# A macaron transformer block on one core: FFN pieces dealt out over the attention rounds by two tables, and the output projection in other PSUM banks

## The reference

```
x = x + 0.5 * ffn(layernorm(x))
x = x + attn(layernorm(x))
x = x + 0.5 * ffn(layernorm(x))

ffn(x)  = (silu(x @ w_gate.T) * (x @ w_up.T)) @ w_down.T          # hidden 2048
attn(x): q, k, v = x @ w_qkv                                      # 16 heads of 32
         q, k = unit norm per head, rope on every other head
         logits = q @ k.T * q_gain, causal mask
         y = softmax(logits) @ v;  return y @ w_out
```

## Time and profile before

| | |
|---|---|
| median of 3 runs | 2855.55 us (2854.16 to 2855.95) |
| the profiled execution | 2854.06 us, of it 2852.1 us from the first to the last instruction |
| PE busy | 2760.0 us, 97% of the span |
| DVE, ACT, POOL busy | 1755.9, 1206.4, 527.0 us |
| granted TensorE clock, mean | 0.995 |
| start of the first `qkv` of rounds 0 to 7 | 189.7, 479.2, 796.2, 1110.0, 1451.9, 1793.8, 2135.7, 2422.0 us |
| start of their second halves | 359.8, 646.1, 947.8, 1286.7, 1628.6, 1970.5, 2302.6, 2593.0 us |

### The profile page before, as it was taken

The page is one execution under the profiler, slowest core; times in us unless marked ns, Lnnn a source line. Parts: engine busy times, 40 slices in busy tenths (PEclk is TensorE's granted clock), DMA queues, the critical chain, the costliest instruction groups (busy, mean ns, idle before and its releaser), DMA issues.

```text
span 2852.1 us, 56217 instructions
## 1 busy us (share of the span) xinstructions
PE 2760.0 (97%) x23232; PEld 2025.0 (71%) x23232; DVE 1755.9 (62%) x4158; ACT 1206.4 (42%) x2250; POOL 527.0 (18%) x820
## 2 busy tenths in 40 slices
PE   5999999999999999999999999999999999999999
PEld 4677766776677776777767777677767766777676
DVE  7765666666656565566656566565656666665643
ACT  5443444354434443444434444344443444344422
POOL 0012132213130301213021120302103031303100
PEclk8999999999999999999999999999999999999999
DMA  6000000000000000000000000000000000000000
GB/s 253 1 16 1 16 1 1 1 16 16 1 1 16 16 1 1 1 16 16 1 1 16 1 16 1 1 16 16 1 16 1 16 1 1 1 16 9 1 9 15
DMA packets 16574, 39.37 MB, mean 14 GB/s; under 512 B 1472, under 2 KB 1472, under 8 KB 15808
## 3 DMA queue, kind: packets, MB, share of 16 engines
q1 hardware_dynamic: 16320, 35.79, 3.5%
HBM read 26.35 MB, written 9.44 MB: 13 GB/s over the span
## 4 chain that ended last, share of the span: by engine, by line
PE 84%; DVE 10%; ACT 3%; issue 2%; POOL 1%; DMA 0%; SPq 0%; ACTq 0%; DVEq 0%
PE psum L1034 24%; PE psum L1036 24%; PE psum L1035 24%; PE psum L1186 2%; PE psum L1163 2%; DVE mneg L928 2%; PE psum L1198 1%; PE psum L1145 1%; DVE arena L876 1%; PE psum L1141 1%; DVE arena L878 1%; PE psum L1057 1%; DVE arena L949 1%; DVE arena L871 1%; PE psum L1164 1%
## 5 line engine op out<-in xcount | busy, mean ns | idle before, releaser
L1034 PE MATMUL psum<-arena,WG 128*128 128x256 f16 x2048 | 559.1, 273 | 4.9 <-DVE arena L878 3.4
L1036 PE MATMUL psum<-arena,WG 128*128 128x256 f16 x2048 | 559.3, 273 | 0.0
L1035 PE MATMUL psum<-arena,WG 128*128 128x256 f16 x2048 | 559.1, 273 | 0.0
L1034 PE MATMUL psum<-arena,WU 128*128 128x256 f16 x2048 | 558.4, 273 | 0.0
L1036 PE MATMUL psum<-arena,WU 128*128 128x256 f16 x2048 | 558.3, 273 | 0.0
L1035 PE MATMUL psum<-arena,WU 128*128 128x256 f16 x2048 | 558.3, 273 | 0.0
L876 DVE SCALAR_TENSOR_TENSOR arena<-arena,psum 128x256 f32<-128x256 f32 x512 | 215.1, 420 | 492.2 <-ACT arena L768 491.2
L768 ACT ACTIVATE arena<-psum,tscale 128x256 f32<-128x256 f32 x512 | 241.9, 472 | 633.1 <-PE psum L1036 632.8
L1034 PE MATMUL psum<-WD,arena 128*128 128x512 f16 x1024 | 388.1, 379 | 3.9 <-DVE arena L882 3.8
L1036 PE MATMUL psum<-WD,arena 128*128 128x512 f16 x1024 | 388.0, 379 | 0.0
L1035 PE MATMUL psum<-WD,arena 128*128 128x512 f16 x1024 | 387.9, 379 | 0.0
(11 more groups left out here) (147 smaller groups left out, 4534.6 us busy)
## 6 DMA issues: line engine op xcount, KB each, us to landing
arena<-in_L_attn_x SPq DMA_DIRECT2D x16, 512.0 KB, 3.8
out<-arena SPq DMA_DIRECT2D x16, 512.0 KB, 2.8
arena<-in_L_ffn_w_gate SPq DMA_DIRECT2D x4, 1024.0 KB, 9.3
arena<-in_L_ffn_w_up SPq DMA_DIRECT2D x4, 1024.0 KB, 7.3
WD<-in_L_ffn_w_down SPq DMA_DIRECT2D x4, 1024.0 KB, 12.3
arena<-in_L_attn_w_qkv SPq DMA_DIRECT2D x1, 3072.0 KB, 22.1
...
```

The costliest lines, as they stand in the source:

```text
L1034: T_.matmul(o, lhs(0), rhs(0), start=first, stop=False)
L1035: T_.matmul(o, lhs(0), rhs(1), start=False, stop=False)
L1036: return T_.matmul(o, lhs(1), rhs(0), start=False, stop=last)
```

## The change

Two things are changed.

1. `projections`, `heads` and `out` take a table w with a number of beats for each of their places, instead of constants. Rounds 0, 1, 6 and 7 (`SHORT`) use `FEW`, the others `MANY`. Before, the heads' places had 1 beat (0.8 in rounds 0 and 7), the prelude's 0.4 of that, the places of the projections 1, 3 (after the last tile) and 2. The stages themselves, their number and their sequence inside the attention are the same; `max_group` only gathers three lines that stood twice.
2. The output projection writes tiles 0 to 3 into banks 2, 0, 1, 2 (`OUT_BANK`) and not 0, 1, 2, 0. The first `qkv` of a round waits for two out residuals before its first matmul and for the third before its 13th (the v part, in bank 1). The `stack turn` that next uses bank 2 now waits for the fourth.

```
-    LOAD, LEFT, PACE, PRELUDE, SCARCE, ENDS = 9, 3, (0, 2, 3, 4), 0.4, 0.8, 3
+    LOAD, LEFT, PACE = 9, 3, (0, 2, 3, 4)
+    SHORT = (0, 1, 6, 7)
+    MANY = {"qk": 1.88, "qk first": 1, "ends": 3, "stack": 2, "v first": 1.25, "turned": 1, "max first": 0.4,
...
+    FEW = {"qk": 1, "qk first": 2, "ends": 2.4, "stack": 2, "v first": 1, "turned": 1, "max first": 0.32,
...
-                fill(1)
+                fill(w["qk"] if t else w["qk first"])
...
-                    fill(ENDS)
+                    fill(w["ends"])
...
         def attention(b):
+            w = FEW if b in SHORT else MANY
             for hf in range(2):
-                projections(b, hf)
-                heads(b, hf, SCARCE if b in (0, B - 1) else 1)
-            out(b)
+                projections(b, hf, w)
+                heads(b, hf, w)
+            out(b, w)
...
+    OUT_BANK = (2, 0, 1, 2)
...
-                V_.scalar_tensor_tensor(out=x_t, in0=ps(t % 3), scalar=unscale[:, 2:3], in1=x_t, op0=ALU.mult, op1=ALU.add).then_inc(s["x2_done"], 1)
+                V_.scalar_tensor_tensor(out=x_t, in0=ps(OUT_BANK[t]), scalar=unscale[:, 2:3], in1=x_t, op0=ALU.mult, op1=ALU.add).then_inc(s["x2_done"], 1)
...
                 elif b:
-                    pe.wait_ge(s["x2_done"], TT * b)
+                    pe.wait_ge(s["x2_done"], TT * (b - 1) + 2)
...
+                if b and hf == 0 and t == 0:
+                    pe.wait_ge(s["x2_done"], TT * (b - 1) + 3)
...
-                if t == 2:
-                    reader[2] = "x2_done", TT * b + 3
+                if t == 3:
+                    reader[2] = "x2_done", TT * b + 4
```

60 lines of the change are left out of this document (31 added, 29 removed).

## The result

| | before | after |
|---|---|---|
| median | 2855.19 us (2854.16 to 2855.95, 4 runs) | 2815.77 us (2814.85 to 2817.38, 4 runs) |
| profiled execution | 2854.06 us, span 2852.1 | 2815.85 us, span 2814.0 |
| PE busy | 2760.0 us, 97% | 2749.1 us, 98% |

The changed kernel takes 0.9862 of the time of the kernel before (95% interval 0.9849 to 0.9876). Of all executions in this document one, of e13, ran at a mean clock of 0.944 and took 2911 us; it is left out.

A forecast was written before the change was run, and what follows sets the result against it. PE, busy 97% of the span, was taken as the bound, leaving its 92 us of idle time and low-clock time to win; terms 6.6 + 4.4 + 8.0 + 2.5 + 0 + 1.4 - 1.9 + 1.7 = 22.7 us gave 2833 us, range 2825 to 2848.

The forecast's parts named there:

- Term 1: Turns of the rounds: six waits of the first qkv for the fourth out residual go, gain 6.6 us.
- Rival B: First qkv at the turns: another late release takes the out residual's place, term 1 lost, 2839.5 us; chance 0.05.
- Term 2: Stack turns in short rounds' second halves: two pieces instead of one remove four waits, gain 4.4 us.
- Term 3: Preludes of short rounds' second halves: residual and norm leave DVE's queue there, PE's waits shrink, gain 8.0 us.
- Terms 4 and 5: Single waits behind layer norms, 2.5 us; heads: 0 to 3 gain 0 on a straight line, 4 to 7 gain 1.4.
- the lower bound: Heads 0 to 3 of the four short rounds: all 2.8 us of idle time gone in each, -11 us.
- term 6: Long rounds: two places in the first half's prelude lose their only piece, costing 1.9 us.
- Term 4's last sentence: Waits of values for a turn's split: four before, four after at other heads, so nothing gained.
- Term 7: Round 1's second half: the one clock fall goes as two waits that meet are moved apart, gain 1.7 us.
- Rival C: Short rounds' first halves: short waits gather and bring more stretches at 1.2 GHz, 2841.5 us; chance 0.06.
- A: Heads 0 to 3, short rounds' first halves: 25 pieces too few to cover DVE, +11 us, 2844 us; chance 0.15.
- D: Heads 0 to 3, four first halves: DVE becomes the bound, 41 us lost, slower kernel at 2874 us; chance 0.05.

The follow-up runs named there:

- e13: Changed kernel with the short rounds' weight for values and values' turns at 0.769 instead of 0.56, exponentials kept at 1.2; 2836.64 us, 0.9939 of the kernel before.
- e1: Kernel before with only the output projection's new banks and the two changed waits, pieces placed as before; 2845.52 us, 0.9968 of the kernel before.
- e5: Changed kernel with other short-round head weights: similar piece counts per group of heads, placed elsewhere inside each head; 2831.1 us, 0.9918 of the kernel before.
- e7: Changed kernel with the short rounds' head weights all 0.3 (18 pieces in heads 0 to 3) and projections at old values; 2866.3 us, 1.0042 of before.
- e4: Changed kernel with the short rounds' six head weights all set to their mean, 0.769; 2837.85 us, 0.994 of the kernel before.
- e10: Changed kernel with more beats for the v part in all rounds (FEW 2, MANY 1.9); 2818.06 us, 0.9873 of the kernel before.

## Why the forecast was right in sign and short in size

**Term 1, the banks: right.** 6 x 1.10 us was the price, 6.6 us the gain, in the changed kernel and in e1. Rival B is out.

**Term 2, the stack turns: right, for half a reason.** The four waits went, 4.4 us; small ones beside them bring it to 5.9. I had reasoned with one piece of 1.23 us against a wait of 1.0 at the last place. Three halves of e13 have that piece and wait all the same: the wait is for the whole way from the last `qkv` over `stack` to `stack turn`, and the pieces on that way count, six before and in e13, eight after. They are there because the first halves took fewer, not because the table says 2.

**Term 3, the preludes: the mechanism right, 1.2 us too much.** DVE's load went where the order said. What is left is 2.0 us in the four (1.2 by the second count), where I had left one wait of 0.31 in three of them. By the second count 8.1 us were there to win and not 8.9: the eight waits were priced too high.

**Terms 4 and 5, the heads: here the forecast failed.** Forecast 3.9 us, measured 14.7, and with that 2815.8 us and not 2833. The step is "on a straight line between the two rows the halves would share the 2.8 us". Two rows, 33 pieces with 0 us idle and 16 with 2.8, do not give a line. What PE loses there is a number of single waits, and each ends when the place ahead of it has enough pieces; 2 pieces were nearly enough ahead of the scores and 1 too few ahead of the next `scores max`, as the table of pieces and e5 show. Both halves therefore end near zero (0.35 and 0.09 us idle in round 6; over the four short rounds 13.2 us lost became 6.2): I had that case as the lower bound, -11 us, and took the middle for no better reason than that it was the middle. The range cut part of that bound off. In heads 4 to 7 I had priced the pieces of round 7 and four single waits, some 3 us, and added nothing for the small waits of the other halves; 7.6 us were won there. Of PE's waits before, those of `y turn` (2.2 us in six) and of `values` for the low halves (1.8 us in four) are not in its list after; what each place of heads 4 to 7 gained was not tried by itself. The two terms make 10.8 of the 16 us by which the gain was forecast too small, term 6 makes 4.2.

**Term 4's last sentence, "four before, four after: nothing", was wrong too.** The four waits of `values` for a split are four, but take 2.6 us and not 4.8. A count of places is not a sum of waits: what stands on DVE ahead of the split sets the length.

**Term 6, the long rounds: wrong sign, a misread order.** I wrote that two places of the first half's prelude lose their only piece. They do not: ahead of the second, third and fourth `scores max` stood 2, 1, 2 pieces, and now 1, 2, 1. The window of round 4's first prelude after shows no idle time.

```profile
1504.30:1518.30 14.00, 14.00 (x116) 10.12 (x115) 9.58 (x26) 2.86 (x6) 0.00 (x0) 1.00 0.00 1
```

What I did not look for is in the heads: the wait of `max rows` for a split, 0.70 us in the second half of each of the four rounds, went, and heads 0 to 3 of both halves won 3.6 us; 1.8 were lost in the second halves' projections, to norm turns. Term 6 should have been +2.3.

**Term 7, the clock: the right sum, by luck.** The 1.7 us came, but e1 gets them with the two waits still together. What decides on a fall stays open. The Trainium skill (TensorE: Matmul & The Clock Gate, section "A second HAM failure mode: psum-queue depth-cycling") says that a PE which idles briefly again and again can swing between the clocks. The traces agree as far as they go: e7, with 81.6 us lost, has five falls of 3.41 us each between 600 and 2700 us, the kernel before with 70.3 has one, the changed kernel none. But the number of falls does not follow the loss alone: e4 and e13, with over 50 us lost, have none, e10 with some 34 has two. Rival C did not come: the changed kernel has no fall between 65 us and its end.

**Rivals A and D** stood on DVE's mean share. A asked for 11 us in the four first halves, which lost 1.8 us more in heads 0 to 3 than before and 2.4 less behind them. D took 0.89 as the share from which on PE idles 25% (12.94 of 14.50 us in round 6's prelude), but the earlier trace rows had the same 0.89 in round 7's, 9.01 of 10.10 us, with 0.14 us idle. A kernel slower than before was found, e7, but it loses most in heads 4 to 7; that DVE bounds heads 0 to 3 of the first halves, as D had it, no run shows.
